# Chunked state-space layers: the output projection and the gate moved into their own chunk, z projected in two halves, the state faded into a buffer

## The reference, cut to what matters

```python
for i in range(N_LAYERS):
    res = h
    h = _layernorm(h, ln_w[i], ln_b[i])
    h = _mamba2(h, ...)
    h = h + res
...
z, xBC, dt = jnp.split(u @ in_w.T, ...)
xBC = silu(conv(xBC, conv_w, 4 taps) + conv_b)
state = dA_t * state + (dt_t * x_t) * B_t      # for each token t
y_t = einsum(state, C_t)
y = (y + D * x) * silu(z)
y = y * rsqrt(mean(y * y, -1) + EPS) * rms_w
return y @ out_w.T
```

## Time and profile before

| | us |
|---|---|
| median of 3 runs (1802.56 to 1810.76) | 1802.65 |
| the profiled execution, its own time | 1809.7 |
| its span, first to last instruction | 1808.1 |
| TensorE / VectorE / ScalarE / GpSimd busy in the span | 1381.9 / 1084.4 / 712.8 / 410.3 |
| mean granted TensorE clock | 0.855 of 2.4 GHz |

### The profile page before, as it was taken

How to read it: one execution, slowest core, us unless ns; L and a number is a source line. 1 busy time by engine, 2 the same in 40 slices (tenths; PEclk the granted TensorE clock), 3 DMA queues, 4 the chain that set the end, 5 groups by cost and what they waited for, 6 DMA issues and landing times.

```text
span 1808.1 us, 33973 instructions
## 1 busy us (share of the span) xinstructions
PE 1381.9 (76%) x12846; PEld 939.4 (52%) x12847; DVE 1084.4 (60%) x1663; ACT 712.8 (39%) x1039; POOL 410.3 (23%) x391
## 2 busy tenths in 40 slices
PE   3726998897478899856399999759679778889791
PEld 1215666564356567624255555527547546666570
DVE  3586677766668767768755555545454544555332
ACT  3245343433643434422421111425466445555330
POOL 0121333443224334321314233040000000000003
PEclk9857889988689989888598998659889898999896
DMA  8051000001200000022210000254443533434004
GB/s 292 2 189 33 2 1 1 1 1 50 98 7 2 1 1 1 1 80 108 79 47 0 0 0 0 96 206 156 153 143 135 194 129 113 158 121 161 14 30 147
DMA packets 34092, 133.28 MB, mean 74 GB/s; under 512 B 6665, under 2 KB 8457, under 8 KB 24017
## 3 DMA queue, kind: packets, MB, share of 16 engines
q1 hardware_dynamic: 25808, 103.17, 15.8%
q0 software_dynamic: 8160, 28.32, 4.6%
HBM read 108.80 MB, written 22.68 MB: 73 GB/s over the span
## 4 chain that ended last, share of the span: by engine, by line
PE 43%; DVE 20%; issue 12%; PEld 8%; ACT 7%; DMA 4%; PEldq 3%; POOL 3%; DVEq 0%; POOLq 0%; ACTq 0%; SPq 0%
PE banks L2037 7%; DVE mb_ca L590 6%; PE banks L2048 6%; PEld banks L2037 6%; PE banks L1601 5%; PE banks L964 4%; PEld banks L2048 2%; PE banks L1678 2%; PE banks L940 2%; PE banks L1031 2%; PE banks L1023 2%; PEldq L1770 2%; PE banks L1654 2%; PE banks L1001 1%; PE banks L1011 1%
## 5 line engine op out<-in xcount | busy, mean ns | idle before, releaser
L2037 PE MATMUL banks<-eb_x_hi,eb_w_hi 128*128 128x128 f16 x1344 | 240.0, 226 | 85.1 <-issue 53.5
L2037 PE MATMUL banks<-eb_x_lo,eb_w_hi 128*128 128x128 f16 x1344 | 239.9, 226 | 0.0
L2037 PE MATMUL banks<-eb_x_hi,eb_w_lo 128*128 128x128 f16 x1344 | 239.4, 225 | 0.0
L940 PE MATMUL banks<-mb_u_hi,mb_wi_hi 128*128 (+3 forms) x1152 | 199.3, 221 | 1.8 <-ACT mb_ca L772 1.8
L940 PE MATMUL banks<-mb_u_hi,mb_wi_lo 128*128 (+3 forms) x1152 | 198.9, 221 | 0.0
L940 PE MATMUL banks<-mb_u_lo,mb_wi_hi 128*128 (+3 forms) x1152 | 198.7, 221 | 0.0
L2037 PEld LDWEIGHTS banks<-eb_x_hi,eb_w_hi 128*128 128x128 f16 x1344 | 136.5, 102 | 90.4 <-issue 88.9
L590 DVE SCALAR_TENSOR_TENSOR mb_ca<-mb_xp,mb_par,mb_ca 128x128 f32<-128x128 f32 x384 | 141.5, 433 | 32.8 <-ACT mb_ca L772 30.3
L2037 PEld LDWEIGHTS banks<-eb_x_lo,eb_w_hi 128*128 128x128 f16 x1344 | 136.4, 102 | 1.5
L2037 PEld LDWEIGHTS banks<-eb_x_hi,eb_w_lo 128*128 128x128 f16 x1344 | 136.6, 102 | 0.0
L2048 PE MATMUL banks<-eb_w_hi,eb_h_hi 128*128 128x512 f16 x336 | 127.3, 379 | 3.1 <-issue 3.1
(11 more groups left out here) (427 smaller groups left out, 3313.8 us busy)
## 6 DMA issues: line engine op xcount, KB each, us to landing
eb_raw<-e_w SPq DMA_DIRECT2D x36, 1024.0 KB, 5.6
eb_un<-e_w SPq DMA_DIRECT2D x28, 1024.0 KB, 6.5
mb_ring<-m_in_w SPq DMA_DIRECT2D x8, 1072.0 KB, 5.3
xs_table<-zero POOLq DMA_DIRECT2D x1, 6400.0 KB, 21.1
eb_xg<-xs_table POOLq DMA_DIRECT2D x23, 256.0 KB, 2.9
ys_table<-eb_y POOLq DMA_DIRECT2D x21, 256.0 KB, 2.3
ab_raw<-a_in_w SPq DMA_DIRECT2D x4, 1154.0 KB, 11.7
mb_ring<-m_out_w SPq DMA_DIRECT2D x4, 1024.0 KB, 5.1
```

The costliest lines, as they stand in the source:

```text
L940: x = e.matmul(ps[0:width, bank, n * P:(n + 1) * P], a[:, k, f:f + width], b[:, k, ds(i * P, P)], start=(k == 0 and m == 0), stop=(k == KD ...
L2037: o = e.matmul(ps[:, j, c * P:(c + 1) * P], a[side][:, k, f * P:(f + 1) * P], b[:, k, :], start=(k == 0 and m == 0), stop=(k == KD - 1 and ...
```

## The change

All of it is order and waits, save that the faded state goes into a part of `ring` instead of S itself. On TensorE the products inside a chunk (L1042) come ahead of the next chunk's projections; behind `project_x` follow the next chunk's growth sums, then the whole output projection and row sum of the same chunk, then the first half of z. The second half of z goes between groups k=1 and k=2 of the next chunk. On VectorE `lower_y` follows L675, `conv` follows that, and the gate's halves stand ahead of k=0 and behind k=7. On ScalarE `upper_y` stands ahead of the evictions of `project_x`, and `square_y` between its two halves. On GpSimd the fade and the D product come first, and `sum_squares` stands ahead of `conv_bc`. The diff, cut to its core:

```diff
+    faded = ring[0:NS, 0:DI]
...
# dve
             def body(i, g, is_first, is_last):
+                if not is_first:
+                    e.wait_ge(y_done, g)
+                gate(g, 0)
                 e.wait_ge(bt_done, g + 1)
                 for k in range(MB_EG):
...
-                    if k == 1 and not is_first:
-                        lower_y(g - 1)
...
+                    if k == 6 and not is_first:
+                        add_rows(i - 1, g - 1)
+                gate(g, 1)
                 e.wait_ge(inter_mm, g + 1)
...
-                if not is_first:
-                    finish(i - 1, g - 1)
                 e.wait_ge(ds_mm, g + 1)
                 e.wait_ge(smul, g + 1)
-                e.tensor_tensor(S[:], S[:], ps[0:NS, 3:5, :].rearrange("p b n -> p (b n)"), ALU.add).then_inc(s_done, 1)
-                if not is_last:
-                    e.wait_ge(dx_done, g + 1)
-                    conv(g + 1)
+                e.tensor_tensor(S[:], faded, ps[0:NS, 3:5, :].rearrange("p b n -> p (b n)"), ALU.add).then_inc(s_done, 1)
+                if not is_first:
+                    row_stats(i - 1, g - 1)
                 e.wait_ge(intra_mm, g + 1)
...
                 e.tensor_tensor(y, y, sz[:], ALU.mult).then_inc(y_done, 1)
+                lower_y(g)
                 if not is_last:
-                    e.wait_ge(y_done, g + 1)
-                    gate(g + 1)
+                    e.wait_ge(dx_done, g + 1)
+                    conv(g + 1, lambda: row_norm(g))
...
# act
             def project_x(g, is_first):
...
                     x.then_inc(x_ev, 1)
+                    if q == 0 and not is_first:
+                        square_y(g - 1)
...
+                else:
+                    grow(g)
                 for q in range(2):
                     e.wait_ge(acc, 2 * g + q + 1)
...
             def body(i, g, is_first, is_last):
+                project_z(g, 0)
                 e.wait_ge(g_mm, g + 1)
...
-                    if not is_first and k == 1:
-                        upper_y(g - 1)
-                    if not is_first and k == 3:
-                        square_y(g - 1)
-                e.wait_ge(ecum_mm, g + 1)
...
+                    if k == 3:
+                        project_z(g, 1)
+                upper_y(g)
                 if not is_last:
                     project_x(g + 1, False)
-                    project_z(g + 1)
...
# pool
             def body(i, g, is_first, is_last):
                 if not is_first:
-                    sum_squares(g - 1)
+                    power(g - 1)
+                    e.wait_ge(s_done, g)
+                    core.apart(e)
+                e.tensor_tensor(heads(faded), heads(S[:]), edec[0:NS, i, :].unsqueeze(2).to_broadcast([NS, H2, 32]),
+                                ALU.mult).then_inc(smul, 1)
                 e.wait_ge(xc_done, 2 * (g + 1))
...
-                e.wait_ge(inter_mm, g + 1)
-                if is_last:
-                    e.sem_inc(ring_free, 1)
...
                 e.tensor_tensor(yi, yi, dx, ALU.add).then_inc(yid_done, 1)
+                if is_last:
+                    e.wait_ge(s_done, g + 1)
+                    core.apart(e)
+                    e.sem_inc(ring_free, 1)
+                sum_squares(g)
                 if not is_last:
                     conv_bc(g + 1)
                     keep_halo(g + 1)
...
# pe
             def body(i, g, is_first, is_last):
                 e.wait_ge(bcc_done, g + 1)
                 if not is_first:
-                    e.wait_ge(ya_done, g)
+                    e.wait_ge(rv_done, g)
...
-                if not is_first:
-                    e.wait_ge(s_done, g)
+                e.wait_ge(ec_done, g + 1)
                 core.apart(e)
                 for k in range(MB_EG):
...
-                    if k >= 4 and not is_first:
-                        out_project(g - 1, 2 * (k - 4), 2 * (k - 3))
...
+                    if k == 1:
+                        project_z(i, g, 1)
                 e.wait_ge(x_scaled, g + 1)
...
                 x.then_inc(inter_mm, 1)
-                if not is_first:
-                    e.wait_ge(m_done, MB_EG * (g + 1))
-                    sum_rows(g - 1)
-                e.wait_ge(ec_done, g + 1)
+                e.wait_ge(exped, MB_EG * (g + 1))
                 for q in range(2):
...
                 x.then_inc(ds_mm, 1)
-                if not is_last:
-                    project_x(i + 1, g + 1, False)
-                if is_first:
-                    e.wait_ge(m_done, MB_EG * (g + 1))
-                else:
+                e.wait_ge(m_done, MB_EG * (g + 1))
+                if not is_first:
                     e.wait_ge(h_done, g)
...
                 x.then_inc(intra_mm, 1)
                 if not is_last:
-                    project_z(i + 1, g + 1)
+                    project_x(i + 1, g + 1, False)
+                    e.wait_ge(s_done, g + 1)
+                    core.apart(e)
+                    growth(i + 1)
+                out_project(g)
+                sum_rows(g)
+                if not is_last:
+                    project_z(i + 1, g + 1, 0)
```

More of the change, by code:

```diff
@@ L602, in conv, with gate, row_norm, add_rows @@
                     .then_inc(bcc_done, 1)
-            def gate(g):
-                for q in range(2):
-                    e.wait_ge(thz_done, 2 * g + q + 1)
-                    e.scalar_tensor_tensor(out=sz[:, 4 * q:4 * q + 4, :], in0=thz[:, 4 * q:4 * q + 4, :], scalar=1.0,
-                                           in1=ps[:, 1 - q, :].rearrange("p (j t) -> p j t", j=4),
-                                           op0=ALU.add, op1=ALU.mult).then_inc(sz_done, 1)
-            def finish(i, g):
+            def gate(g, q):
+                e.wait_ge(thz_done, 2 * g + q + 1)
+                e.scalar_tensor_tensor(out=sz[:, 4 * q:4 * q + 4, :], in0=thz[:, 4 * q:4 * q + 4, :], scalar=1.0,
+                                       in1=ps[:, 1 - q, :].rearrange("p (j t) -> p j t", j=4),
+                                       op0=ALU.add, op1=ALU.mult).then_inc(sz_done, 1)
+            def row_norm(g):
                 e.wait_ge(rms_mm, g + 1)
                 e.tensor_scalar(rv[:], ps[:, 2, 384:385], 1.0 / DI, 4 * MB_EPS, ALU.mult, ALU.add).then_inc(rv_done, 1)
+            def add_rows(i, g):
                 e.wait_ge(pow_done, g + 1)
@@ L689, in dve @@
             body(TT - 1, l * TT + TT - 1, False, True)
-            lower_y(l * TT + TT - 1)
             with e.If(l > LAYERS - 2):
@@ L912, in pool @@
             chunks(e, l, body)
-            sum_squares(l * TT + TT - 1)
             power(l * TT + TT - 1)
@@ L951, in project_x, with project_z, growth, out_project @@
                 project(i, 0, [MB_CB, MB_CC], NS, bc_mm)
-            def project_z(i, g):
-                e.wait_ge(x_ev, 2 * g + 2)
-                project(i, 1, [P * j for j in range(4)], P, z_mm)
-                e.wait_ge(bc_ev, g + 1)
-                project(i, 0, [P * j for j in range(4, 8)], P, z_mm)
-            def out_project(g, first, end):
+            def project_z(i, g, q):
+                if q == 0:
+                    e.wait_ge(x_ev, 2 * g + 2)
+                else:
+                    e.wait_ge(bc_ev, g + 1)
+                project(i, 1 - q, [P * j for j in range(4 * q, 4 * q + 4)], P, z_mm)
+            def growth(i):
+                for j in range(JD):
+                    x = e.matmul(ps[:, 3 + j // 4, (j % 4) * P:(j % 4 + 1) * P], sel[:, j, :], cum[0:MB_CR, ds(i * P, P)],
+                                 start=True, stop=True)
+                x.then_inc(ecum_mm, 1)
+            def out_project(g):
                 e.wait_ge(ylo_done, g + 1)
-                for j in range(first, end):
+                for j in range(JD):
                     for m, (a, b) in enumerate(((y_hi, wo_hi), (y_hi, wo_lo), (y_lo, wo_hi))):
@@ L965, in out_project @@
                                      stop=(j == JD - 1 and m == 2))
[L966 to L967 removed]
+                x.then_inc(out_mm, 1)
             def sum_rows(g):
@@ L987, in pe @@
             e.wait_ge(ones_set, 1)
+            growth(0)
             def body(i, g, is_first, is_last):
```

45 lines of the change are left out of this document (18 added, 27 removed).

## The result

| | before | changed |
|---|---|---|
| runs beside each other, median (lowest to highest), us | 1805.91 (1802.56 to 1810.76), 4 runs | 1855.81 (1850.74 to 1875.32), 4 runs |
| ratio, 95% interval | | 1.0302 (1.0251 to 1.0352) |
| again, unedited (the last experiment) | 1807.67, 11 runs | 1861.90, 6 runs; ratio 1.0305 (1.0256 to 1.0354) |
| profiled execution: time, span, us | 1809.70, 1808.1 | 1855.46, 1853.9 |
| one inner chunk, mean of 12, us | 35.77 | 39.74 |

The change makes the kernel 3.0% slower: 50 us by the medians, where +49 was forecast. As the stages show, the nearness is in part luck.

The account below looks back on a forecast made before the run. No engine alone bounds the kernel; a chunk's TensorE-VectorE loop does. Inner chunks +3.3 us, times 12: +40; first chunks +12; last chunks −3; sum +49, median 1802.65 to 1851 us, range 1801 to 1880.

Parts of the forecast that it names:

- case A: The forecast itself, whole kernel: slower by 49 us, median 1851 us, range within it 1829 to 1880; chance 0.58.
- Steps 1 and 2: Chunk's groups: z's half delays M number 2 to +8.4; without output projection there, state product at +13.3, gain only 1.1 us.
- Step 4: Products inside the chunk ahead of the projection: 1.9 us new on the path, `project_x` at +19.1 against +18.09.
- Step 5: y rounded ahead of the evictions on ScalarE: convolution at +24.8, 5.7 us behind the projection instead of 4.92.
- Step 6: Convolution: GpSimd's sums of squares beside the 24 taps stretch them by 1.5 us (bounds 0 and 2.5); next chunk at +37.5.
- Step 7: Low TensorE clock in the middle of a chunk, around the state product: 1.6 us more, bounds 0 and 3.2.
- Step 3: Growth sums ahead cost nothing behind `project_x`; the faded buffer, whose fade no longer waits for L1023, put at 0.
- The rule beside the row: VectorE taps with two SBUF inputs fully blocked by GpSimd: squares cost 2.5 us instead of 1.5, 14 times, 1865 us.
- B: Rival: TensorE keeps 2.4 GHz through the groups, so the middle's low-clock cost goes; 1824 us, chance 0.15.
- C: Rival: warm throughout, gap before a chunk too short for the clock to fall; 1808 us, shares a chance of 0.13.
- D: Rival: C, and GpSimd's squares cost the taps nothing, 1.5 us off 14 chunks; 1787 us, chance 0.14.

Follow-up runs that it names:

- b_intra: Kernel before, with only the next chunk's projection of x put behind the products inside the chunk; ratio 1.0192 to the kernel before, inner chunk 38.09 us.
- a_sq: Changed kernel, with TensorE adding all eight blocks of squares and GpSimd's sums gone; ratio 1.0231 to the kernel before, inner chunk 36.97 us.
- b_pool: Kernel before, with three more GpSimd additions beside the taps, results unused; ratio 1.0172 to the kernel before, inner chunk 37.54 us.
- a_warm: Changed kernel, with idle products behind groups 2 to 7, eight of them behind the last; ratio 1.0154 to the kernel before, inner chunk 36.86 us.
- b_warm: Kernel before, with ten idle products in TensorE's gap ahead of a chunk, run twice; ratios 0.986 and 0.9931 to the kernel before, inner chunk 33.81 us.
- a_gap: Changed kernel, with nine idle products only in TensorE's gap ahead of a chunk; ratio 1.0306 to the kernel before, inner chunk 38.51 us.
- a_z: Changed kernel, with z's second half back ahead of the chunk, right behind the first; ratio 1.0067 to the kernel before, inner chunk 37.43 us.
- c_z4sq: Changed kernel, z's second half in quarters behind groups 2 to 5, eight idle products, squares on TensorE; ratio 0.9941 to the kernel before, inner chunk 32.97 us.

## Why the prediction came out

The direction and the forecast case A were right. The time was right as well, but by luck in part: the sum for the stage that changed was 16 us too small, and the expert stage, put at 0, was 19 us shorter in the profile. By its steps, for the chunk at 672.10:

*Steps 1 and 2 held.* M number 2 is at +7.85 (forecast +8.4), L1036 at +12.65 (+13.3). *Step 4 held*: `project_x` is at +19.91, against 19.1 + 1.6 with the low clock, and b_intra shows the 1.9 for the order, with 0.8 more of a wait that the changed kernel doesn't have. *Step 5 held*: the convolution at +25.62 is 5.71 behind `project_x` (forecast 5.7). y was rounded ahead of the evictions (timeline of ScalarE):

```profile
694.74 1.06 ACT L817 ACTIVATE mb_y_hi<-mb_quad 128x1024 f16<-128x1024 f32 x1 [10.49 <-DVE mb_quad L681]
695.71 0.59 ACT L782 ACTIVATE mb_xp<-banks 128x512 f32<-128x512 f32 x1
```

No run took the rounding away, so its +0.8 rests on these rows. *Step 6 held*: taps 10.96, +1.67 (forecast 1.5), shown by a_sq and b_pool; the next chunk at +38.5 (37.5 + 1.6).

*Step 7 failed in size.* The low clock in the middle was put at 1.6 us a chunk, so 5.80 + 1.6 = 7.4 from L1036 to `project_x`. It took 7.26 in the shortest chunks, 8.87 in the ones of 40.07 and 8.27 in the mean, 0.9 more than forecast; in a_warm, at the high clock, it takes 5.56, so the low clock cost 2.7. The other steps together came out 0.2 lower, hence 3.97 instead of 3.3, 12 times: 8 of the 16 us. The step took the smaller of its two samples because L1042 "now stands between"; that product ran at the low clock as well (331 ns for 274).

*Step 3 failed in one place.* The faded buffer was put at 0 by looking for who waits for the fade, and nobody does. But the fade now runs right at a chunk's opening, before the products of x, and in a layer's first chunk it meets L603, on which TensorE waits. VectorE and GpSimd at that place in the changed kernel:

```profile
168.87 3.98 DVE L603 SCALAR_TENSOR_TENSOR mb_bcc<-mb_thbc,mb_cbc 32x256 f32<-32x256 f32 x1
```

```profile
168.33 2.39 POOL L907 TENSOR_TENSOR mb_ring<-mb_S,mb_edec 32x1024 f32<-32x1024 f32 x1
170.69 1.89 POOL L910 TENSOR_TENSOR mb_quad<-mb_xc,mb_par 128x1024 f32<-128x1024 f32 x1
```

L603 took 3.98 instead of 0.41 us, and ends 0.27 behind GpSimd's two instructions; the same row stands at 546.83 in layer two. That is the 3.5 us ahead of layer one's first chunk, and as much was lost at layer two's opening. These are seven more of the 16 us. It is read from the traces; no run moved the fade. The last chunk of layer one gained 2.2 up to its gate (L681 21.39 behind its first instruction, before 23.58) and 0.8 more on the way to layer two, so that of the 3.6 only 0.6 is left in that row, where −1.4 was forecast.

*The first chunks* were put at 5.8 each and came out at 4.2 and 8.8: the sum of both is nearly right, 13.0 for 11.6, each of them is not. The middle took 7.25 in layer one's and 10.05 in layer two's. *The last chunk* of layer two gained 2.0 up to its gate (L681 21.37 behind its first instruction, before 23.37) and gave it back by the next stage's first product; why stays open. What is left of the 16 us is about one: 1.4 more in the first chunks and 1.5 in layer two's last, 1.6 less in layer one's.

*The rule beside the row.* The forecast went by 0.62 of GpSimd's time, and the full block of the Trainium skill (SBUF — State Buffer, "Who interferes with whom") was put at 2.5 us. The taps lost 1.67 for 2.62 us (0.64) in one kernel and 1.77 for 2.47 (0.72) in the other. By the trace it is nonetheless a block, taken GpSimd instruction by GpSimd instruction. The line of the taps, in the chunk from 697 to 710:

```profile
L590 DVE SCALAR_TENSOR_TENSOR mb_ca<-mb_xp,mb_par,mb_ca x24: 339/348/1243, 697.7 to 708.3; 128x128 f32<-128x128 f32 x24
```

The middle tap has its 348 ns. The three beside GpSimd's sums stand 1243, 882 and 614 ns, and each ends some 0.15 us behind the end of a sum. The sums themselves took 1.28, 0.73 and 0.46 us, as in the kernel before, where no tap stood beside them: the sums are not slowed, and VectorE loses their time less one tap of its own for each sum. L603 did not get through between GpSimd's two instructions: it lost 3.6 us of the 3.7 for which they still ran; why, is not shown. The Trainium skill's rule holds in kind; how much is lost depends on how many VectorE instructions get done in between.

*The rivals.* B (warm in the middle), C and D are out: a period below 38 us nowhere, taps at 10.96, two stretches at 0.50 a chunk. What C and D rested on is real, though. The low clock at the opening costs 1.96 us a chunk in the kernel before (b_warm); C had put it at 1.3.

## What to carry to other kernels

Where the engine that sets the pace is handed between TensorE and VectorE, don't put a block of 2.8 us between the first and the second piece that the other engine waits for; cut it into parts and put each behind a piece that runs ahead (39.74 to 34.49 us a chunk, together with idle products for the clock). Before moving work off the path, ask what clock the engine will have afterwards: taking the output projection from between the groups left gaps of 0.3 and 2.2 us and with them a second cold stretch, and dropping eight idle products cost 0.9 us a chunk (which the whole time doesn't show). And list what runs on GpSimd beside each VectorE instruction that someone waits for, even where nobody waits for GpSimd.

## What the runs showed of the hardware that was not expected

- An idle gap of 3.03 us each 35.8 us cost 1.96 us a chunk in TensorE's clock; ten products that nobody reads in that gap bought it back, twice with the same 33.81 us.
- A warm opening made the middle colder: L1036 went from 335 to 396 ns in a_gap, where nothing but the opening was warmed, so the gains of two cold stretches don't add. (412 ns in a_z, where z's half had left the groups as well.)
- One VectorE instruction of 0.41 us stood 3.98 us behind two GpSimd instructions in a row.
- The expert stage varied from 573 to 614 us over 14 profiles, with TensorE busy 468 to 472 us in all of them, and by 17 us between two profiles of b_warm. The median of the runs less the profiled start of the stage, an estimate, is 591 to 595 us for the kernel before and 576 and 582 for the changed one. So a comparison of kernels by the whole time alone would have given a_gap no gain and c_z4sq a third of its own (11 of 34 us).
